# A four-layer graph network on one core: weight loads issued behind the first chunks of x, and the last chunk finished in two halves

## What is computed

```python
x = _layernorm(x + h @ W_self + (adj @ h / deg) @ W_neigh)        # h = x, deg = clip(sum(adj, 1), 1)
x = _layernorm(x + relu(adj @ (x @ kernel) + bias))
x = _layernorm(x + relu(adj @ (relu(adj @ (x @ W1) + b1) @ W2) + b2))
x = _layernorm(x + swish(adj @ swish(adj @ x @ W + b) @ W + b))   # W and b of L3
```

## Time and profile before

| | us |
|---|---|
| median of three runs | 1157.9 |
| lowest, highest | 1157.37, 1159.23 |
| the profiled execution, its own time | 1157.31 |
| its span in the trace | 1155.1 |
| TensorE busy | 1135.4 (98%) |
| VectorE, ScalarE, GpSimd busy | 825.4, 553.0, 69.6 |

### The profile page before, as it was taken

One profiled execution on the slowest core, in us unless ns is written; L12 is line 12 of the kernel. 1 busy time (PEld: TensorE's weight loads), 2 busy tenths in 40 slices (PEclk: granted clock), 3 DMA queues, 4 the chain that ended last, 5 costly groups with the idle time before them and its releaser, 6 DMA issues.

```text
span 1155.1 us, 13921 instructions
## 1 busy us (share of the span) xinstructions
PE 1135.4 (98%) x4964; PEld 894.5 (77%) x4964; DVE 825.4 (71%) x1105; ACT 553.0 (48%) x626; POOL 69.6 (6%) x48
## 2 busy tenths in 40 slices
PE   8999999999999999999999999999999999999995
PEld 3455667777788888888888888888888888888884
DVE  4888889799799666595445498566577545668885
ACT  1112324444565444474444474444366444657774
POOL 0000000000121111000000010000000000000110
PEclk9999999999999999999999999999999999999998
DMA  8988666565768656496655487655668665788883
GB/s 320 361 285 285 234 226 229 210 234 186 278 251 298 214 192 215 172 342 234 215 194 202 171 301 266 220 205 203 218 216 317 204 210 197 252 318 296 297 287 120
DMA packets 82625, 279.43 MB, mean 242 GB/s; under 512 B 8832, under 2 KB 14208, under 8 KB 82560
## 3 DMA queue, kind: packets, MB, share of 16 engines
q1 hardware_dynamic: 75744, 273.71, 67.6%
q10 hardware_dynamic: 6816, 4.85, 1.4%
HBM read 276.43 MB, written 2.10 MB: 241 GB/s over the span
## 4 chain that ended last, share of the span: by engine, by line
PE 96%; DMA 1%; DVE 1%; ACT 1%; issue 0%; SPq 0%; DVEq 0%; ACTq 0%
PE acc L435 27%; PE acc L440 26%; PE acc L436 26%; PE acc L423 12%; PE acc L472 4%; DMA raw<-adj_tiles 1%; PE acc L450 1%; PE acc L458 0%; DVE adj_lo L699 0%; DVE deg_part L603 0%; ACT t_x L541 0%; DMA out<-t_x 0%; DVE stats L614 0%; DVE t_y L646 0%; ACT adj_hi L583 0%
## 5 line engine op out<-in xcount | busy, mean ns | idle before, releaser
L699 DVE TENSOR_TENSOR adj_lo<-raw,adj_hi 128x1024 fp32r<-128x1024 f32 x419 | 509.5, 1230 | 252.3 <-ACT adj_hi L583 237.9
L583 ACT CAST adj_hi<-raw 128x1024 fp32r<-128x1024 f32 x419 | 438.5, 1051 | 397.0 <-PE acc L440 246.1
L435 PE MATMUL acc<-adj_hi,op_hi 128*128 128x512 f32 x1336 | 529.0, 396 | 0.9 <-ACT t_aux L513 0.9
L436 PE MATMUL acc<-adj_hi,op_lo 128*128 128x512 f32 x1336 | 520.4, 390 | 0.0
L440 PE MATMUL acc<-adj_lo,op_hi 128*128 128x512 f32 x1336 | 411.7, 389 | 0.2 <-DVE adj_lo L699 0.2
L435 PEld LDWEIGHTS acc<-adj_hi,op_hi 128*128 128x128 f32 x1336 | 251.0, 188 | 54.4 <-issue 2.6
L436 PEld LDWEIGHTS acc<-adj_hi,op_lo 128*128 128x128 f32 x1336 | 251.0, 188 | 53.0 <-issue 2.6
L440 PEld LDWEIGHTS acc<-adj_lo,op_hi 128*128 128x128 f32 x1336 | 250.7, 188 | 53.2 <-DVE adj_lo L699 0.6
L603 DVE TENSOR_TENSOR deg_part<-deg_part,raw 128x1024 f32<-128x1024 f32 x120 | 146.5, 1221 | 14.4 <-DMA raw<-adj_tiles 9.4
L423 PE MATMUL acc<-raw,x_rows 128*128 128x512 f32 x312 | 140.5, 603 | 5.7 <-DMA raw<-adj_tiles 5.7
L722 POOL TENSOR_TENSOR rstd<-var_eps,minus_half 128x4 f32<-128x4 f32 x32 | 57.1, 1785 | 1070.6 <-DVE var_eps L619 1070.6
(11 more groups left out here) (48 smaller groups left out, 292.4 us busy)
## 6 DMA issues: line engine op xcount, KB each, us to landing
raw<-adj_tiles SPq DMA_DIRECT2D x518, 512.0 KB, 4.8
x_rows<-x_blocks SPq DMA_DIRECT2D x8, 256.0 KB, 6.5
xt<-x_t ACTq DMA_DIRECT2D x8, 256.0 KB, 5.4
out<-t_x ACTq DMA_DIRECT2D x8, 256.0 KB, 4.9
w<-W ACTq DMA_DIRECT2D x2, 64.0 KB, 8.3
b<-b ACTq DMA_DIRECT2D x2, 64.0 KB, 11.3
w_res<-W_self ACTq DMA_DIRECT2D x1, 64.0 KB, 3.5
w_neigh<-W_neigh ACTq DMA_DIRECT2D x1, 64.0 KB, 4.6
```

Of the source, the lines that this page charges most:

```text
L435: nc.tensor.matmul(bank, op_block(op_hi, p, j), a_hi, start=first and b == 0, stop=False)
L436: nc.tensor.matmul(bank, op_block(op_lo, p, j), a_hi, start=False, stop=False)
L583: nc.scalar.copy(split_hi(s), raw[:, g % RAW, :]).then_inc(hi_ready, 1)
L699: nc.vector.tensor_tensor(split_lo(s), raw[:, g % RAW, :], split_hi(s).bitcast(fp32), ALU.subtract).then_inc(lo_ready, 1)
```

## The change

**Start.** ACT's first work is the cast of x's chunks. W_self, W_neigh and the first `xt` are issued behind the third cast, the other eight small loads behind the eighth, on a semaphore of their own (`w_rest_loaded`), for which pass 1 waits. DVE adds the identity to W_self at step 16 instead of 4. `ROWS_AT` moves every `rows_of_x` later.

**Order in pass 0.** `SELF_AT` and `SCALE_AT` change places: ACT scales chunk m ahead of copying the rows product of chunk m + 1, where it was behind. A few other entries move by one to eight eighths of a step.

**End.** For the last chunk (`FINAL`, m = 47) all steps run on halves of two blocks, with semaphores of their own. ACT copies two halves; TensorE puts the bias into the bank by a product of the identity with the broadcast bias (256 columns), adds the weight products, and does so for two banks; Silu reads the bank; DVE and POOL make moments and rstd for each half; DVE subtracts the mean and multiplies, into `xt` (free since pass 0) instead of `t_x`; SP issues a store for each half.

```diff
     ROWS_AT = [
-        11, 17, 39, 50, 64, 84, 108, 128
+        21, 36, 47, 62, 81, 105, 125, 153
     ]
...
     SELF_AT = [
-        426, 432, 436, 502, 598, 756, 822, 974
+        428, 433, 437, 509, 605, 757, 853, 981
     ]
...
     SCALE_AT = [
-        433, 437, 510, 606, 757, 853, 981, 1110, None, None, None, None, None, None, None, None, None, None,
+        432, 436, 508, 604, 756, 852, 980, 1110, None, None, None, None, None, None, None, None, None, None,
...
+            c = FINISH[FINAL][1]
+            for h in range(2):
+                sp.wait_ge(last_norm_ready, 2 * h + 2)
+                row = c * CW + h * 2 * P
+                sp.dma_start(out[row:row + 2 * P, :].rearrange("(b p) d -> p b d", p=P),
+                             rows4(xt)[:, 2 * h:2 * h + 2, :]).then_inc(last_stored, 16)
+            sp.wait_ge(last_stored, 32)
...
+            def last_rows(m):
+
+                for h, user in enumerate((("z", m), ("second", m))):
+                    bank = take(user)
+                    nc.tensor.matmul(bank[:, 0:2 * D].rearrange("p (b d) -> p b d", b=2), ident[:],
+                                     B_OF[LAST][:].unsqueeze(1).broadcast_to([P, 2, D]), start=True, stop=False)
+                    pe.wait_ge(last_agg_out, h + 1)
+                    for b in range(2):
+                        j = 2 * h + b
+                        last = nc.tensor.matmul(bank[:, b * D:(b + 1) * D], t_agg[:, m % 2, j * P:(j + 1) * P], W_OF[LAST][:],
+                                                start=False, stop=b == 1)
+                    last.then_inc(last_z_done, 1)
...
+            def last_silu(m):
+                for h, user in enumerate((("z", m), ("second", m))):
+                    half = slice(h * 2 * D, (h + 1) * 2 * D)
+                    act.wait_ge(last_z_done, h + 1)
+                    if h == 0:
+                        act.wait_ge(y_ready, BPC * CHUNKS + m - 3 * CHUNKS)
+                    nc.scalar.activation(t_aux[:, half], acc[:, BANK[user], 0:2 * D], ACT.Silu).then_inc(last_silu_ready, 1)
...
-            for dst, src in WEIGHTS[:2]:
-                act.dma_start(dst, src).then_inc(w_loaded, 16)
-            xt_load(0)
-            for dst, src in WEIGHTS[2:]:
-                act.dma_start(dst, src).then_inc(w_loaded, 16)
-
             for u in range(END * PARTS):
                 if u in X_HI_AT:
-                    split_x(X_HI_AT.index(u))
+                    k = X_HI_AT.index(u)
+                    split_x(k)
+                    if k == 2:
+                        for dst, src in WEIGHTS[:2]:
+                            act.dma_start(dst, src).then_inc(w_loaded, 16)
+                        xt_load(0)
+                    if k == CHUNKS - 1:
+                        for dst, src in WEIGHTS[2:]:
+                            act.dma_start(dst, src).then_inc(w_rest_loaded, 16)
...
-                if g == 4:
+                if g == W_RES_STEP:
                     dve.wait_ge(ident_ready, 1)
-                    dve.wait_ge(w_loaded, 16 * len(WEIGHTS))
+                    dve.wait_ge(w_loaded, 32)
```

More of the change, by code:

```diff
@@ L219, in bass_gnn_residual_norm_kernel @@
     ]
+    W_RES_STEP = 16
+    FINAL = PASSES * CHUNKS - 1
     END = max(u for u in SCALE_AT + NORM_AT if u) // PARTS + 1
@@ L231, in bass_gnn_residual_norm_kernel @@
         users += [("z", m) for m in range(PASSES * CHUNKS) if (DEGREES_AT + WEIGHT_AT[CHUNKS:])[m] == at]
+        users += [("second", m) for m in range(PASSES * CHUNKS) if m == FINAL and WEIGHT_AT[m] == at]
         users += [("sum", FINISH_NO[key]) for key in SUM_OF[at:at + 1] if BEGUN[key] == at]
@@ L235, in bass_gnn_residual_norm_kernel @@
             kind, m = user
-            until = {"rows": at + 4, "z": WEIGHT_AT[m] + 4, "sum": ENDED[FINISH[m]] + 3}[kind]
+            until = {"rows": at + 4, "z": WEIGHT_AT[m] + 4, "second": at + 4, "sum": ENDED[FINISH[m]] + 3}[kind]
             held.append((until, BANK[user], user))
@@ L507, in sum_out, with last_sum_out @@
                 nc.scalar.copy(t_agg[:, m % 2, :], acc[:, BANK["sum", m], :]).then_inc(agg_out, 1)
+            def last_sum_out(m):
+                act.wait_ge(f_done, F_COUNT[m])
+                act.wait_ge(z_done, m - 1)
+                for h in range(2):
+                    half = slice(h * 2 * P, (h + 1) * 2 * P)
+                    nc.scalar.copy(t_agg[:, m % 2, half], acc[:, BANK["sum", m], half]).then_inc(last_agg_out, 1)
+            def last_silu(m):
[5 more added lines that the diff above has]
+                    nc.scalar.activation(t_aux[:, half], acc[:, BANK[user], 0:2 * D], ACT.Silu).then_inc(last_silu_ready, 1)
             def self_rows(m):
@@ L518, in after @@
                 p, c = FINISH[m]
+                if m == FINAL:
+                    if u == SUM_AT[m]:
+                        last_sum_out(m)
+                    if u == SILU_AT[m]:
+                        last_silu(m)
+                    return
                 if u == SUM_AT[m]:
@@ L712, in _ @@
             pool.wait_ge(half_ready, 1)
-            for m in range(len(NORM) * CHUNKS):
+            for m in range(len(NORM) * CHUNKS - 1):
                 if CHUNKS <= m < 2 * CHUNKS:
```

78 lines of the change are left out of this document (66 added, 12 removed), and 8 rows, old and new, of tables (BIAS_AT, NORM_AT, SCALE_AT, SUM_AT).

## The result

| | before | changed |
|---|---|---|
| median of four runs, us | 1158.57 | 1150.07 |
| lowest, highest | 1157.37, 1159.24 | 1149.44, 1151.11 |
| the profiled execution, its own time | 1157.31 | 1149.44 |
| its span in the trace | 1155.1 | 1147.3 |

The ratio of the times is 0.9928, with a 95% interval of 0.9915 to 0.9940. The forecast was 1151.4 with a range of 1149.7 to 1154.0. The spans differ by 7.8 us; the sum of the forecast had 5.9. So 1.9 us have to be found, and most of the study is about these and about what the single edits are worth alone.

What follows compares the result with a forecast made beforehand. TensorE's work was taken to bound the middle, leaving gains at the edges and one gap: 0.3 start + 0.9 gap + 4.7 end = 5.9 us off the profiled 1157.31, so 1151.4 us; range 1149.7 to 1154.0.

Steps and rivals of the forecast that it cites:

- The start: Ahead of TensorE's first product: moving small loads behind casts starts it 0.45 us sooner, 0.3 of which reaches the end.
- near 5.3: Sign at the start: the first product begins near 5.3 us, against 5.72 before.
- the two choices on the clock: TensorE's clock rise at the start: as long behind the start as before (0.45 us won), or same moment (0.22).
- Records of 0.83 up to about 11: Sign at the start: TensorE's records take 0.83 us each, at the lower clock, up to about 11 us.
- The moved loads: Small loads among raw loads, around 50 us: cost nothing, at most 1 us, against 2.4 us of slack.
- The gap: Pass 0 near 260 us: TensorE's 0.9 us wait for ACT's rows copy goes; gap or a new one 0.13.
- The end: Behind the last large product: 9.3 instead of 14.0 us to the span's end, saving 4.7, bounds 3.7 to 5.3.
- the other branch: DVE and POOL at the end: second rstd near 1147.0, two DVE scalings to 1147.7, store landed at 1150.0.
- ACT's branch: At the end: four scalings of the chunk before the last to 1147.35, store of 2.30 us, landed at 1149.65.
- The slower one: Rival: with the exchanged ACT order TensorE waits 5.0 us for each of seven chunks, 35 us, time 1187; chance 0.02.
- twenty steps at least: Pass 0: each rows bank's next user stands at least twenty steps, 30 us, behind its rows product.

Runs made afterwards that it cites:

- the small products: Changed kernel with eight products of the identity with itself on TensorE ahead of the first raw tile: 1148.84 us, ratio 0.9917.
- end alone: Kernel before with only the change's new end; small loads first and tables of before: 1153.58 us, ratio 0.9960.
- rows alone: Kernel before with one table changed, the later steps of the eight rows products: 1165.20 us, ratio 1.0062.
- rows and casts: Fifth in order: kernel before with later rows products, ACT's first copy behind the sixth cast and one cast moved ahead: 1158.52 us, ratio 1.0000.
- other buffer: Kernel before with the last chunk's four scalings going into `xt` and stored from it; no halves, bias on VectorE: 1156.53 us, ratio 0.9983.
- the last run: Changed kernel with eight identity products ahead of the first raw tile and an earlier shift of the chunk before the last: 1147.75 us, ratio 0.9912.
- one table entry: Changed kernel with one `NORM_AT` entry less by one, making the shift of the chunk before the last sooner: 1148.84 us, ratio 0.9919.

## Why the prediction was right, point by point

**The start (0.3, bounds 0 to 1.0).** The first product came at 5.30, as forecast ("near 5.3"). Over the traces, the four with late loads and without the small products start at 5.30 to 5.52 (mean 5.38), the seven with loads first at 5.60 to 5.88 (mean 5.70): 0.32. But the two traces with the small products have late loads too and start at 5.53 and 5.87; with them the difference of the means is 0.21, and the ranges overlap. Of the two choices on the clock, rise with the start or at a fixed moment, the trace took neither: 2.8 us sooner than before. "Records of 0.83 up to about 11" was wrong in that execution and nearly right in the second one (10.25). The bound of 1.0 did not hold the 1.5 us that this trace shows for first product and rise together.

**The moved loads (nothing, at most 1 us).** Right: no wait of TensorE for a raw tile behind the first. The prediction named VectorE's 5.2 us wait for the last bias and gave its removal no value. It has one: where that wait stood, TensorE stopped near 27 us in three of five traces for 0.8 to 1.2 us from record to record (end alone, rows alone, rows and casts), and in none of the eight with the wait moved. That it cost nothing in the profiled execution of before was luck, and may be a part of why the medians differ by 8.5 and the traces by 7.8.

**The gap (0.9).** It goes, and is 1.2 us where measured from record to record: a weight load lies open behind the wait. In other executions of the old order it is 0.4 (end alone) and 1.7 (other buffer). The prediction priced a chance size from one trace. Whether removing it by the table alone brings anything the fifth run leaves open.

**The end (4.7, bounds 3.7 to 5.3).** 4.92. Behind the last large product, forecast against measured: first Silu done 1.60 and 1.60; variance of the first half done 2.99 and 3.06; of the second 4.37 and 4.39; ACT's scalings begin 4.52 and 4.49. The step that failed is the other branch. It was to be the last: rstd stretched by VectorE to 1.44 and 1.31 us, scalings done 6.57 us behind the last large product, the store landed at 8.87. Measured: both rstd took 0.80, the scalings end at 5.90, and the second half store lands 1.86 us behind its issue, at 7.8. ACT's branch ended the program, and its store took 2.5 us where 2.30 was taken, so the sum came out nearly right with the wrong engine in front. That is luck in the size of the end, though not in its main piece, the wait for `t_x`.

The prediction quoted from the Trainium skill (GPSIMD Engine Reference, Specifications) the contention of GpSimd with VectorE instructions of two SBUF inputs. The traces agree, and show how much it is. Two rstd of the kernel before, beside the same VectorE subtraction of 512 columns (`op_lo`, L677):

```profile
332.44 0.68 DVE L677 TENSOR_TENSOR op_lo<-x_rows,op_hi 128x512 fp32r<-128x512 f32 x1
332.62 1.39 POOL L722 TENSOR_TENSOR rstd<-var_eps,minus_half 128x4 f32<-128x4 f32 x1 [3.79 <-DVE var_eps L619]
...
691.61 1.01 POOL L722 TENSOR_TENSOR rstd<-var_eps,minus_half 128x4 f32<-128x4 f32 x1 [4.23 <-DVE var_eps L619]
691.65 0.71 DVE L677 TENSOR_TENSOR op_lo<-x_rows,op_hi 128x512 fp32r<-128x512 f32 x1
```

The subtraction that was running when the rstd began cost it 0.38 us; the one that began 0.04 us later cost nothing. In the thirteen traces of the table, all 372 rstd of four columns that began beside a running VectorE instruction with two tiles as inputs ended 0.86 to 0.88 us past its end; the 23 that began with no VectorE instruction running took 1.01 us, whatever began beside them. So what is added is the rest of the instruction already running. The prediction added whole lengths (0.43 and 0.3) instead, and took the 1.01 us of four columns where a half has two. The halves were not free of the effect: the first began with 0.25 us of VectorE's addition left, the second with 0.24 us of a scaling left (one tile as input), and both ended 0.55 us past that; in the last run, with 0.17 left, the second took 0.72.

The fixed part that the Trainium skill gives for a DMA (DMA: Bandwidth & Descriptors, Anatomy of one DMA), about 2.0 us, is stated there for DMAs issued by GpSimd. The half stores, issued by SP, took 1.8 to 1.9 us in all; that a half isn't half of 2.3 the prediction has right. Its remark that by this figure the sum would not change is wrong by its own numbers: the branches would have landed at 1149.7 and 1149.65 instead of 1150.0, and the end would have come 0.3 us sooner.

**The rivals.** The slower one (the exchanged order, 1187) did not come: ACT waits 8.7 us for the rows products and TensorE never for ACT. But its mechanism is real in the mirror image. Moving the rows products without moving ACT's casts costs 7 us, by a copy that holds the casts, VectorE and a raw buffer. The prediction followed the banks ("twenty steps at least") and not the casts behind the copy.

## What to carry to other kernels

An operation that is made later for one engine drags along whatever stands behind its consumer on the next: move it only with a look at the rows that the waiting instruction holds, as the run of one table shows (7 us for a wait of 1). In an end where two branches finish side by side, measure both to the landing of their stores; the branch that I thought safe set the time, and one table entry then gave another 1 us. And a difference of 1 to 2 us between two traces may be the start alone: repeat the same program before you give it a cause. Where GpSimd works beside VectorE, price what is left of the VectorE instruction that runs at the start, not the length of those that follow.

## What the runs showed of the hardware

The moment at which TensorE's clock goes from 1.2 to 2.4 GHz at the start (seen in the distance of records, and in the first entry of the granted clock's record) lies between 3.3 and 6.1 us behind the first large product, and differs by 1.5 us between two executions of one program. With TensorE busy from 1.52 us on it still came at 8.0 and 10.2 us. The medians gain 1.3 and 1.1 us by the eight small products (1150.17 to 1148.84, 1148.84 to 1147.75); that this is an earlier rise in most executions is likely but not shown, since one trace of the two has it and the other not.

A small GpSimd operation (rstd, 1.01 us by itself) that begins while a VectorE instruction with two tiles as inputs runs ends 0.86 to 0.88 us behind that instruction, up to 1.93 us long; one that VectorE begins later does not slow it.

At the end, with no other load under way, a store of 128 KB from SP's queue took 1.8 to 1.9 us to land, one of 256 KB on ACT's queue 2.30, and 2.5 where both of SP's had been issued ahead of it.
